# The closing recurrence of a hybrid block: 16 images as one chain of sigmoid steps, or as two chains of 8 issued in turn

## The reference

```python
def _L1_ffn_ref(x, W, V, gamma, beta):          # x: (16, 4096, 128) after a layer norm
    Wx = jnp.einsum('bti,hi->bth', x, W)
    Wx = batchnorm_over_all_rows(Wx) * gamma + beta
    def step(yt, wx_t):
        yt = jax.nn.sigmoid(wx_t + yt @ V.T)
        return (yt, yt)
    _, ys = jax.lax.scan(step, zeros((16, 128)), jnp.swapaxes(Wx, 0, 1))
    return jnp.swapaxes(ys, 0, 1)
t = t + _L1_ffn_ref(...)
```

## Time and profile before

| what | value |
|---|---|
| median of 3 runs | 6170.18 us (6168.44 to 6174.66) |
| span of the profiled execution | 6164.3 us |
| PE busy | 5726.0 us, 102096 matmuls and 102096 weight loads |
| ACT busy | 3194.6 us |
| DVE busy | 2970.5 us |
| POOL busy | 1771.3 us |
| instruction queue q8 | 807 packets, 13.22 MB |

### The profile page before, as it was taken

The page is one execution under the profiler, slowest core; times in us unless marked ns, Lnnn a source line. Parts: engine busy times, 40 slices in busy tenths (PEclk is TensorE's granted clock), DMA queues, the critical chain, the costliest instruction groups (busy, mean ns, idle before and its releaser), DMA issues. The chain is left out here.

```text
span 6164.3 us, 243586 instructions
## 1 busy us (share of the span) xinstructions
PE 5726.0 (93%) x102096; PEld 3455.4 (56%) x102096; DVE 2970.5 (48%) x7682; ACT 3194.6 (52%) x9230; POOL 1771.3 (29%) x2114
## 2 busy tenths in 40 slices
PE   5599999997899997999999997999999999999999
PEld 4499888995666665965455554333333333333333
DVE  8577667774877775558888887000000000000000
ACT  5455555564666665358888886333333333333333
POOL 2000000003777773038888887000000000000000
PEclk7799999999999999999999998999999999999999
DMA  8631112125777772237777775111111111111111
GB/s 361 271 111 56 56 56 81 57 83 202 236 223 231 230 217 86 59 103 222 220 220 221 219 221 152 31 46 47 45 47 45 54 51 47 45 46 45 47 47 44
DMA packets 853671, 751.72 MB, mean 122 GB/s; under 512 B 70256, under 2 KB 731760, under 8 KB 849520
## 3 DMA queue, kind: packets, MB, share of 16 engines
q1 hardware_dynamic: 836944, 634.49, 34.4%
q0 software_dynamic: 14208, 101.45, 4.1%
q10 hardware_dynamic: 1440, 0.33, 0.0%
HBM read 425.72 MB, written 308.45 MB: 119 GB/s over the span
## 5 line engine op out<-in xcount | busy, mean ns | idle before, releaser
L2407 PE MATMUL f_junk<-f_idle 128*32 128x384 bf16 x24736 | 1567.1, 323 | 2.0 <-issue 1.7
L2450 ACT ACTIVATE f_y<-f_acc 128x16 f32<-128x16 f32 x4096 | 749.6, 183 | 1558.2 <-PE f_acc L2418 1558.2
L2418 PEld LDWEIGHTS f_acc<-f_y,f_vT 128*32 128x32 f32 x32768 | 649.8, 108 | 1412.9 <-ACT f_y L2450 1400.5
L2418 PE MATMUL f_acc<-f_y,f_vT 128*32 128x16 f32 x32768 | 1050.7, 193 | 59.1 <-issue 10.3
L2365 DVE TENSOR_TENSOR f_sum<-f_turned,f_t 128x512 f32<-128x512 f32 x128 | 88.5, 692 | 1768.3 <-PE f_turned L2400 1768.2
L2407 PEld LDWEIGHTS f_junk<-f_idle 128*32 128x32 bf16 x24736 | 447.7, 96 | 3.6 <-issue 3.5
L2125 DVE TENSOR_REDUCE o_m<-o_bank_l 128x8 f32<-128x512 f32 x512 | 329.5, 685 | 185.1 <-PE o_bank_l L1903 183.5
L524 POOL DMA_DIRECT2D hidden<-l_h x48 | 36.1, 754 | 1200.5 <-DVE l_hsum L724 972.8
L1161 ACT ACTIVATE a_p<-a_s 128x512 f32<-128x512 f32 x512 | 264.0, 603 | 147.6 <-PE a_s L1046 147.6
L647 ACT ACTIVATE l_gate<-l_pf,l_bf 128x256 f32<-128x256 f32 (+7 forms) x512 | 201.8, 445 | 239.2 <-PE l_pf L574 214.7
L2083 ACT ACTIVATE o_p<-o_bank_s 128x512 f32<-128x512 f32 x512 | 264.3, 603 | 84.9 <-PE o_bank_s L1924 84.9
(11 more groups left out here) (277 smaller groups left out, 11976.0 us busy)
## 6 DMA issues: line engine op xcount, KB each, us to landing
o_v<-vals SPq DMA_DIRECT2D x256, 272.0 KB, 3.4
a_hid<-hidden SPq DMA_DIRECT2D x112, 520.0 KB, 4.7
hidden<-l_h POOLq DMA_DIRECT2D x48, 1040.0 KB, 6.3
skew<-gn_skew POOLq DMA_DIRECT2D x8, 6144.0 KB, 23.1
l_x<-skew SPq DMA_DIRECT2D x46, 1024.0 KB, 5.2
vals<-a_v SPq DMA_DIRECT2D x128, 272.0 KB, 3.4
gn_x<-in_x SPq DMA_DIRECT2D x16, 2048.0 KB, 15.6
a_xin<-in_x SPq DMA_DIRECT2D x128, 256.0 KB, 4.5
```

Source lines behind the costliest of these rows:

```text
L2407: nc.tensor.matmul(junk[rows, :], idle[:, 0:QUAD], idle[:, :], start=True, stop=True)
L2418: mm = nc.tensor.matmul(acc[k % 2][rows, t, :], vT[:, rows], before, start=False, stop=True, skip_group_check=True)
L2450: nc.scalar.activation(y[q][:, u, :], acc[u // RC % 2][:, u % RC, :], ACT.Sigmoid).then_inc(s_y, 1)
```

## The change

The 16 images are dealt to two trains of 8 (`TRAINS`, `LPT`), each with accumulators, a product semaphore and a sigmoid semaphore of its own. For each token PE now issues: the product of train 0, one piece of other work (a `lay` of one train, a `turn`, or one `keep_warm`), the product of train 1, and always one `keep_warm`. ACT has two sigmoids of 8 columns for each token in place of one of 16. `FILL` goes from 384 to 320 columns. A chunk is 64 tokens and not 32, so that an accumulator of 8 images fills the same PSUM space; there are 16 pieces of `lay` and 16 of `turn` in a block as before, each of 128 columns as before. One semaphore that was used once is merged into another.

```diff
-RC = 32
+RC = 64
-FILL = 384
+FILL = 320
+TRAINS = 2
+LPT = B // TRAINS
...
-        acc = [m.ps(f"f_acc{k}", [C, RC, B]) for k in range(2)]
+        acc = [[m.ps(f"f_acc{h}{k}", [C, RC, LPT]) for k in range(2)] for h in range(TRAINS)]
...
+            def step(T, q, u, h):
+                k, t = u // RC, u % RC
+                pe.wait_ge(s_y[h], RT * T + u + 1)
+                before = y[q][:, u - 1, train[h]] if u else y[1 - q][:, RT - 1, train[h]]
+
+                for g in range(P // QUAD):
+                    rows = slice(QUAD * g, QUAD * g + QUAD)
+                    mm = nc.tensor.matmul(acc[h][k % 2][rows, t, :], vT[:, rows], before, start=False, stop=True,
+                                          skip_group_check=True)
+                mm.then_inc(s_mm[h], 1)
+
             def body(T, q, first, last):
                 for u in range(RT):
                     k, t = u // RC, u % RC
-
-                    pe.wait_ge(s_y, RT * T + u + 1)
-                    before = y[q][:, u - 1, :] if u else y[1 - q][:, RT - 1, :]
-
-                    for g in range(P // QUAD):
-                        rows = slice(QUAD * g, QUAD * g + QUAD)
-                        mm = nc.tensor.matmul(acc[k % 2][rows, t, :], vT[:, rows], before, start=False, stop=True,
-                                              skip_group_check=True)
-                    mm.then_inc(s_mm, 1)
+                    step(T, q, u, 0)
                     spare = True
-                    if t % 2 == 0 and t // 2 < PIECES and not (last and k == CHUNKS - 1):
+                    if t % 2 == 0 and t // 2 < TRAINS * PIECES and not (last and k == CHUNKS - 1):
                         spare = False
+                        h, piece = t // 2 % TRAINS, t // 2 // TRAINS
                         if k < CHUNKS - 1:
-                            lay(T, q, k + 1, t // 2)
+                            lay(T, q, k + 1, h, piece)
...
-                    if not first and 2 * PIECES <= t < 2 * PIECES + 16 and t % 4 == 0:
+                    if not first and first_turn <= t < first_turn + 4 * turns and t % 4 == 0:
                         spare = False
-                        turn(T - 1, 1 - q, b)
+                        turn(T - 1, 1 - q, turns * k + (t - first_turn) // 4)
                     if spare:
                         keep_warm()
-                        keep_warm()
+                    step(T, q, u, 1)
+                    keep_warm()
...
                 for u in range(RT):
-                    act.wait_ge(s_mm, RT * T + u + 1)
-                    nc.scalar.activation(y[q][:, u, :], acc[u // RC % 2][:, u % RC, :], ACT.Sigmoid).then_inc(s_y, 1)
+                    for h in range(TRAINS):
+                        act.wait_ge(s_mm[h], RT * T + u + 1)
+                        nc.scalar.activation(y[q][:, u, train[h]], acc[h][u // RC % 2][:, u % RC, :], ACT.Sigmoid
+                                             ).then_inc(s_y[h], 1)
```

More of the change, by code:

```diff
@@ L2257, in recurrence_phase @@
         s_bn = sems.sem("f_bn")
-        s_rstd = sems.sem("f_rstd")
         s_wx = [sems.sem(f"f_wx{q}") for q in range(2)]
@@ L2262, in recurrence_phase @@
         s_pre = sems.sem("f_pre")
-        s_mm = sems.sem("f_mm")
-        s_y = sems.sem("f_y")
+        s_mm = [sems.sem(f"f_mm{h}") for h in range(TRAINS)]
+        s_y = [sems.sem(f"f_y{h}") for h in range(TRAINS)]
+        train = [slice(LPT * h, LPT * h + LPT) for h in range(TRAINS)]
         s_turn = sems.sem("f_turn")
@@ L2331, in _ @@
             pool.wait_ge(s_bn, 2)
-            pool.tensor_tensor(rstd[:, :], vare[:, :], half[:, :], ALU.pow).then_inc(s_rstd, 1)
+            pool.tensor_tensor(rstd[:, :], vare[:, :], half[:, :], ALU.pow).then_inc(s_const, 1)
         @block.vector
@@ L2336, in _ @@
             dve.sem_inc(s_sum, SUM0)
-            nc.vector.memset(y[1][:, RT - 1, :], 0.0).then_inc(s_y, 1)
+            for h in range(TRAINS):
+                nc.vector.memset(y[1][:, RT - 1, train[h]], 0.0).then_inc(s_y[h], 1)
             nc.vector.bn_aggr(mv[:, :], wx_stats[:, :, :].rearrange("c b (k s) -> c (b k) s", s=6)).then_inc(s_bn, 1)
@@ L2342, in _ @@
             dve.wait_ge(s_w, 48)
-            dve.wait_ge(s_rstd, 1)
+            dve.wait_ge(s_const, 5)
             nc.vector.tensor_tensor(scale[:, :], rstd[:, :], gam[:, :], ALU.mult).then_inc(s_bn, 1)
@@ L2380, in _, with lay @@
             pe.wait_ge(s_const, 4)
-            def lay(T, q, k, piece):
-                if piece == 0 and k == 0:
+            def lay(T, q, k, h, piece):
+                if piece == 0 and k == 0 and h == 0:
                     pe.wait_ge(s_norm, T + 1)
@@ L2388, in lay @@
                     rows = slice(QUAD * g, QUAD * g + QUAD)
-                    mm = nc.tensor.matmul(acc[k % 2][rows, PT * piece:PT * piece + PT, :], ident[:, rows], wxn[q][:, at, :],
+                    mm = nc.tensor.matmul(acc[h][k % 2][rows, PT * piece:PT * piece + PT, :], ident[:, rows], wxn[q][:, at, train[h]],
                                           start=piece == 0, stop=False, skip_group_check=True)
-                if piece == PIECES - 1:
+                if piece == PIECES - 1 and h == TRAINS - 1:
                     mm.then_inc(s_pre, 1)
@@ L2411, in body @@
                     k, t = u // RC, u % RC
-                    pe.wait_ge(s_y, RT * T + u + 1)
-                    before = y[q][:, u - 1, :] if u else y[1 - q][:, RT - 1, :]
-                    for g in range(P // QUAD):
-                        rows = slice(QUAD * g, QUAD * g + QUAD)
-                        mm = nc.tensor.matmul(acc[k % 2][rows, t, :], vT[:, rows], before, start=False, stop=True,
-                                              skip_group_check=True)
-                    mm.then_inc(s_mm, 1)
+                    step(T, q, u, 0)
                     spare = True
-                    if t % 2 == 0 and t // 2 < PIECES and not (last and k == CHUNKS - 1):
+                    if t % 2 == 0 and t // 2 < TRAINS * PIECES and not (last and k == CHUNKS - 1):
                         spare = False
+                        h, piece = t // 2 % TRAINS, t // 2 // TRAINS
                         if k < CHUNKS - 1:
-                            lay(T, q, k + 1, t // 2)
+                            lay(T, q, k + 1, h, piece)
                         else:
-                            lay(T + 1, 1 - q, 0, t // 2)
-                    b = 4 * k + (t - 2 * PIECES) // 4
-                    if not first and 2 * PIECES <= t < 2 * PIECES + 16 and t % 4 == 0:
+                            lay(T + 1, 1 - q, 0, h, piece)
+                    first_turn = 2 * TRAINS * PIECES
+                    turns = B // CHUNKS
+                    if not first and first_turn <= t < first_turn + 4 * turns and t % 4 == 0:
                         spare = False
-                        turn(T - 1, 1 - q, b)
+                        turn(T - 1, 1 - q, turns * k + (t - first_turn) // 4)
                     if spare:
                         keep_warm()
-                        keep_warm()
+                    step(T, q, u, 1)
+                    keep_warm()
             for piece in range(PIECES):
-                lay(0, 0, 0, piece)
+                for h in range(TRAINS):
+                    lay(0, 0, 0, h, piece)
             each_pair(pe, body)
-            pe.wait_ge(s_y, TOK + 1)
+            for h in range(TRAINS):
+                pe.wait_ge(s_y[h], TOK + 1)
             for b in range(B):
```

## The result

The changed kernel takes 7018.26 us (median, 7014.66 to 7029.85), the kernel before 6169.31 us beside it. The ratio is 1.1378 with a 95% interval of 1.1363 to 1.1393: 849 us slower. Forecast were 6925 us in a range of 6600 to 7130.

What follows compares the result with a forecast made beforehand. PE's instruction supply was taken to bound the changed kernel: 814 packets at 3.70 us plus 50 us for data make 3062 us for 2307.9, so +754 and 6925 us in all, range 6600 to 7130.

Steps and rivals of the forecast that it cites:

- What bounds the kernel before: In the recurrence: one closed loop of product, sigmoid and next weight load, 0.56 us for each of 4096 tokens.
- packets of 256 instructions: On DMA queue q8: PE's instructions arrive 256 at a time, one packet lasting 7.76 tokens or 4.33 us before the change.
- one in use and one ahead: At PE's instruction supply: PE holds two packets and asks for the next only when it moves on.
- The latency loop: In each token's product and sigmoid: 8 columns shorten the loop to 0.545 us, at most 53 us gained over 4096 tokens.
- PE's array at nothing: In one token on PE: dearest case 0.54 us fits inside 0.545, so priced at nothing, upper bound 41 us.
- The instructions: PE's supply in the recurrence: 814 packets instead of 526, each taking 3.70 us where 2.74 was needed; 3012 us.
- 50 us for data: Beside block loads: data DMA delays four packets in each of 32 blocks by 0.4 us, 50 us in all.
- Rival 1, fetches keep pace: PE's supply: packets arrive in under 2.74 us, so the 0.545 us loop decides; 6117 or 6158 us, chance 0.08.
- Rival 2, a shorter second part: PE's supply: half the 1.32 us from resumption to next packet start drops out, 3.04 us a packet; 6387 us, chance 0.10.
- Rival 3, the clock: On PE: standing still about 1 us in 3.7 drops the clock to 1.2 GHz; 7180 us in all, chance 0.10.

## Why the prediction was right

**What bounds the kernel before.** Right. One train's latency loop was the bound with 4.33 us of work over a packet; packets of 256 instructions are borne out by the 256 between two pauses and by the runs with 3, 4 and 8 fillers. That PE holds one in use and one ahead fits all of them, but no run varies it.

**The latency loop.** Right, and worth nothing here. The sigmoid of 8 columns took 178 ns (176 forecast), tokens between pauses 0.545 us. That this would not be worth anything stood in the sum, which has no term for it.

**PE's array at nothing.** Right: 128 columns more in each filler moved the time by 8 us, less than the scatter. The slack that took them up was PE's wait for the sigmoid.

**The instructions.** The mechanism and the count were right: 814 packets forecast, 815 seen. The size was a little low: a packet took 3.88 us on the mean where 3.70 and 50 us for data made 3.76. Counted in the trace of the changed kernel, 613 distances in which no data packet starts were 3.79 us on the mean and the 201 others 4.16; so 0.09 x 814 = 73 us were missing in the quiet time and 0.37 x 201 - 50 = 24 in the loads, which is the whole miss of 93 us and a little more. 3.70 had been read from one pause and from a run of four distances in another part of the program. In the changed kernel the quiet distances scatter from 3.5 to 4.15 us (5% to 95%), so one pause says little. The kernel before had not much more to offer: of its 21 clear pauses only one other had under 100 data packets beside it, with 3.82 us between the packets (4861.87 to 4865.69), and over all 21, nearly all of them beside loads, the mean was 4.07. The size was thus a near miss with some luck in it; that the time would grow by hundreds of microseconds did not depend on luck, since even the shortest distance of 3.45 us is far over the 2.74 that the latency loop needed.

**Rival 1, fetches keep pace,** which the rule of the Trainium skill (Runtime: NRT & Kernel Launch, Instruction fetch mechanics) on hidden fetches would have given: fell. It needed a packet in 2.74 us; with PE held up by nothing else a packet took 3.88. **Rival 2, a shorter second part:** fell; the part from resumption to next start, 1.32 in the pause of before, was 1.2 to 1.3 us on the mean in the changed kernel and no shorter in any other. **Rival 3, the clock:** fell for this kernel. The mean of 0.99 hides 19 short stretches at 1.2 GHz, 79 us in all, but packets that touch them took 3.93 us and the others 3.88, so next to nothing was lost. With wide fillers and with eight small ones the clock did drop for long: the danger is real, though not here.

## What to carry to other kernels

Count an engine's instructions for each unit of time, not only its busy time: here PE is supplied with 256 in 3.9 us, some 66 a us, and small tiles in a latency-bound loop reach that before the array is full. The check is quick: multiply the step time by 66 and compare it with the instructions of a step. Idle time with releaser "issue" in the middle of a group of like instructions, together with the packets of the instruction queue, tells it apart from a late semaphore, and 256 instructions from one pause to the next settle it. Two independent chains in turn don't shorten a loop in which each element still takes one round of the same latency (0.545 us between pauses against 0.56); they only add instructions, from 65,520 weight loads to 102,276 in this recurrence.

## What was not expected of the hardware

Each change between matmuls of 32 and of 128 output rows cost about 0.1 us on an otherwise full-clock PE, by an estimate from one kernel (0.42 us for a half token). And once the granted clock had fallen to 1.2 GHz in a pause of 4.18 us, it stayed there under a PE that showed as busy all the time, 2300.00 of 2300.00 us, with fillers 128 rows wide. With fillers in narrow matmuls it came back within some 7 us in the kernel before, and the changed kernel, with the same columns in four narrow matmuls, held 0.99. What makes the difference is open.
